# Expert stages: normalisation on ScalarE, bias additions behind the weighted row, and the first tile's work reordered

## The reference

```python
x = x + 0.5 * _L0_ffn_ref(_layernorm(x), gate_w, base_w, base_b, lora_A, lora_B)
x = x + _L0_attn_ref(_layernorm(x), wq, wk, wv, wo)
x = x + 0.5 * _L0_ffn_ref(_layernorm(x), gate_w, base_w, base_b, lora_A, lora_B)
x = x + 0.5 * _L1_ffn_ref(_layernorm(x), W_gate, W_up, W_down)       # SwiGLU
x = x + _L1_attn_ref(_layernorm(x), ...)                             # Mamba2
x = x + 0.5 * _L1_ffn_ref(_layernorm(x), W_gate, W_up, W_down)
```

```python
gate_logits = jnp.einsum('bsd,ed->bse', x, gate_w)            # 8 experts
weights, selected = jax.lax.top_k(gate_logits, 2)
weights = jax.nn.softmax(weights, axis=2)
result = jnp.einsum('bsd,od->bso', x, base_w) + base_b
w_full = jnp.sum(one_hot(selected, 8) * weights[..., None], axis=2)
low = jnp.einsum('bsd,erd->ebsr', x, lora_A)                  # rank 16
lora_out = jnp.einsum('ebsr,eor,bse->bso', low, lora_B, w_full)
return result + 2.0 * lora_out
```

## Time and profile before

| | us |
|---|---|
| median of 3 runs (2285.08 to 2288.72) | 2286.21 |
| the profiled execution | 2288.39 |
| its span in the profile | 2286.6 |
| first expert stage, to the first attention product | 0 to 80.1 |
| attention | 80.1 to 323.7 |
| second expert stage, to the first SwiGLU product | 323.7 to 384.3 |
| SwiGLU, Mamba2, SwiGLU | 384.3 to 2286.6 |
| TensorE, VectorE, ScalarE, GpSimd busy | 2165, 1704, 1416, 1045 |

### The profile page before, as it was taken

How to read it: one execution, slowest core, us unless ns; L and a number is a source line. 1 busy time by engine, 2 the same in 40 slices (tenths; PEclk the granted TensorE clock), 3 DMA queues, 4 the chain that set the end, 5 groups by cost and what they waited for, 6 DMA issues and landing times. The chain is left out here.

```text
span 2286.6 us, 34632 instructions
## 1 busy us (share of the span) xinstructions
PE 2165.4 (95%) x12541; PEld 1756.7 (77%) x12556; DVE 1703.8 (75%) x2693; ACT 1415.5 (62%) x3062; POOL 1045.4 (46%) x759
## 2 busy tenths in 40 slices
PE   6879978999999999999999999999999999997999
PEld 6756667888778878787887887887888788785887
DVE  7767767232688889889889889888988988986221
ACT  3267743333678776777767767776777677673332
POOL 4366544444144454435534634444544453455442
PEclk9899999999999999999999999999999999998999
DMA  3000010333233223322423323322332333231332
GB/s 129 1 1 1 1 42 24 93 92 92 85 137 107 97 84 139 120 84 84 143 88 111 106 96 113 120 84 99 128 116 84 113 114 116 84 108 39 94 93 83
DMA packets 64152, 202.52 MB, mean 89 GB/s; under 512 B 7024, under 2 KB 8048, under 8 KB 55664
## 3 DMA queue, kind: packets, MB, share of 16 engines
q1 hardware_dynamic: 63984, 200.31, 25.4%
HBM read 197.39 MB, written 2.88 MB: 88 GB/s over the span
## 5 line engine op out<-in xcount | busy, mean ns | idle before, releaser
L526 POOL TENSOR_TENSOR wAl<-rawA,wAh 128x512 fp32r<-128x512 f32 x233 | 326.9, 1415 | 411.2 <-ACT wAh L652 410.6
L1567 PE MATMUL ps<-xTh,wAh 128*128 128x512 f32 x1512 | 428.2, 405 | 7.4 <-DVE oacc L1397 3.0
L1567 PE MATMUL ps<-xTl,wAh 128*128 128x512 f32 x1512 | 417.1, 397 | 0.0
L1567 PE MATMUL ps<-xTh,wAl 128*128 128x512 f32 x1512 | 415.6, 396 | 0.0
L1292 DVE SCALAR_TENSOR_TENSOR work<-ps,chp,work 128x510 f32<-128x510 f32 (+2 forms) x465 | 343.3, 743 | 50.8 <-ACT work L804 40.7
L1567 PEld LDWEIGHTS ps<-xTl,wAh 128*128 128x128 f32 x1512 | 285.9, 189 | 70.0
L1567 PEld LDWEIGHTS ps<-xTh,wAl 128*128 128x128 f32 x1512 | 285.4, 189 | 69.8
L1567 PEld LDWEIGHTS ps<-xTh,wAh 128*128 128x128 f32 x1512 | 277.2, 189 | 78.3 <-issue 17.3
L532 POOL TENSOR_TENSOR wBl<-rawB,wBh 128x512 fp32r<-128x512 f32 x108 | 142.3, 1331 | 385.6 <-ACT wBh L656 385.6
L841 ACT ACTIVATE eb<-eb,gc 128x128 f32<-128x128 f32 x1008 | 307.7, 391 | 17.3 <-DMA eb<-scr_decays 17.3
L576 POOL TENSOR_TENSOR sqt<-gt 128x512 f32<-128x512 f32 x112 | 155.1, 1385 | 120.0 <-DVE gt L1351 112.1
(11 more groups left out here) (202 smaller groups left out, 3976.3 us busy)
## 6 DMA issues: line engine op xcount, KB each, us to landing
eb<-scr_decays SPq DMA_DIRECT2D x63, 1536.0 KB, 6.5
rawA<-ma_in SPq DMA_DIRECT2D x144, 256.0 KB, 3.7
rawA<-fa_in SPq DMA_DIRECT2D x88, 256.0 KB, 2.6
rawB<-mb_in SPq DMA_DIRECT2D x64, 256.0 KB, 2.9
rawB<-fb_in SPq DMA_DIRECT2D x44, 256.0 KB, 2.6
x<-x_in SPq DMA_DIRECT2D x8, 256.0 KB, 6.5
x_out<-x SPq DMA_DIRECT2D x8, 256.0 KB, 2.6
wqraw<-wqkv_in SPq DMA_DIRECT2D x1, 1536.0 KB, 11.1
```

The lines of the kernel that those rows point to most:

```text
L526: nc.gpsimd.tensor_tensor(wAl[:, slot, :], rawA[:, slot, :], wAh[:, slot, :].bitcast(F32), ALU.subtract).then_inc(A_lo, 1)
L1567: return nc.tensor.matmul(o, l, r, start=start, stop=end, **kw)
```

## The change

- In both expert stages the normalisation moves from VectorE to ScalarE. VectorE keeps `shift`, which writes minus mean times `brs` (one element a partition, L1085 of the new file) into `bsh`; ScalarE's `normalise` (L645) computes `brs` times x plus `bsh` with `Identity`. `SHIFTS` counts the shifts of the layers before. `last_norm` and the old `shift` become calls of these. Where VectorE still normalises later tiles itself (attention, SwiGLU), it first waits once for `ln_norm`.
- GpSimd's bias addition also waits for `l0_lw` of its tile, and so everything behind it does.
- First tile: VectorE takes the slices of `w0l` as their high parts come, with the statistics of tile 1 between the third and fourth; TensorE runs the first tile's passes against `w0h` and `w0l` slice by slice, and the transposes of tile 1 stand ahead of its last pass. The split of `lbl` on GpSimd waits for `w0_lo`. The attention's constants (`identb`, `negb`) are made in step 1 instead of ahead of the loop.

```diff
         for t in range(3):
             layer_rstd(0, t)
+        pool.wait_ge(w0_lo, KC)
         split_lo(0, lbl[:, :], lb_raw[:, :], lbh[:, :])
...
                     pool.wait_ge(ln_norm, 8 * k + t + 1)
+                    pool.wait_ge(l0_lw, 8 * i + t + 1)
                     nc.gpsimd.tensor_tensor(x[:, t, :], x[:, t, :], bh[:, :], ALU.add).then_inc(l0_bias, 1)
...
+        def normalise(k, t):
+            a, n = t % 2, 8 * k + t
+            act.wait_ge(ln_shift, SHIFTS[k] + t + 1)
+            if n >= 2:
+                act.wait_ge(ln_tp, n - 1)
+            nc.scalar.activation(work[:, a, :], x[:, t, :], ACT.Identity, bias=bsh[:, a:a + 1],
+                                 scale=brs[:, a:a + 1]).then_inc(ln_norm, 1)
...
+        w0_split(0)
+        normalise(0, 0)
+        w0_split(1)
+        layer_hi(0, 0, 1)
+        w0_split(2)
+        w0_split(3)
+        normalise(0, 1)
...
         def experts(i, k):
-            for t in range(-1, NT + AHEAD - 1):
-                if t + 1 < NT + AHEAD and (k, t) != (0, -1):
-                    layer_hi(*ln_tile(k, t + 1), 1)
+            if i == 1:
+                normalise(k, 0)
+                normalise(k, 1)
+                layer_hi(k, 0, 1)
+            for t in range(NT + AHEAD - 1):
+                layer_hi(*ln_tile(k, t + 1), 1)
+                if t + 2 < NT + AHEAD:
+                    normalise(*ln_tile(k, t + 2))
                 if 0 <= t - 1 < NT:
...
+                if i == 0 and t == 1:
+                    attention_constants()
...
+        def shift(k, t):
+            a, n = t % 2, 8 * k + t
+            dve.wait_ge(ln_rstd, n + 1)
+            if n >= 2:
+                dve.wait_ge(ln_norm, n - 1)
+            nc.vector.tensor_scalar(bsh[:, a:a + 1], bmv[:, a, 0:1], brs[:, a:a + 1], -1.0, ALU.mult,
+                                    ALU.mult).then_inc(ln_shift, 1)
...
+            def statistics(k, t):
+                if 8 * k + t >= 2:
+                    dve.wait_ge(ln_norm, 8 * k + t - 1)
+                layer_stats(k, t)
+
+            statistics(k, 0)
+            if i == 0:
+                shift(0, 0)
+                w0_rest(0)
+                w0_rest(1)
+                layer_lo(0, 0, 1)
+                w0_rest(2)
+                statistics(0, 1)
+                w0_rest(3)
+                shift(0, 1)
+            else:
+                statistics(k, 1)
+                shift(k, 0)
+                shift(k, 1)
+            statistics(k, 2)
+            if i == 1:
+                layer_lo(k, 0, 1)
+            for t in range(NT + AHEAD - 1):
+                if t + 2 < NT + AHEAD:
+                    shift(*ln_tile(k, t + 2))
+                layer_lo(*ln_tile(k, t + 1), 1)
+                if t + 3 < NT + AHEAD:
+                    statistics(*ln_tile(k, t + 3))
...
+                        if early and n < KC:
+                            pe.wait_ge(w0_hi, kc + 1)
+                        elif early and n < 2 * KC:
+                            pe.wait_ge(w0_lo, kc + 1)
+                        elif early and n == 2 * KC:
+                            pe.wait_ge(ln_lo, 1)
+                        if early and n == 2 * KC:
+                            layer_transpose(k, 1, 1, True)
```

More of the change, by code:

```diff
@@ L635, in layer_hi, with w0_split, attention_constants @@
                                  ACT.Copy).then_inc(ln_hi, 1)
-        for kc in range(KC):
+        def normalise(k, t):
[5 more added lines that the diff above has]
+                                 scale=brs[:, a:a + 1]).then_inc(ln_norm, 1)
+        def w0_split(kc):
             act.wait_ge(w0_s[kc], 16)
             nc.scalar.activation(w0h[:, kc, :], w0raw[:, kc, :], ACT.Copy).then_inc(w0_hi, 1)
-            if kc == 1:
-                layer_hi(0, 0, 1)
+        def attention_constants():
+            nc.scalar.activation(identb[:, :], ident, ACT.Copy).then_inc(act_step, 1)
+            for j in range(4):
+                nc.scalar.activation(negb[:, j, :], cst[:, C_NEG:C_NEG + P], ACT.Copy).then_inc(act_step, 1)
+        w0_split(0)
[5 more added lines that the diff above has]
+        normalise(0, 1)
         act.wait_ge(lb_s, 16)
         nc.scalar.activation(lbh[:, :], lb_raw[:, :], ACT.Copy).then_inc(wres_hi, 1)
-        act.wait_ge(cst_in_s, 16)
-        nc.scalar.activation(identb[:, :], ident, ACT.Copy).then_inc(act_step, 1)
-        for j in range(4):
-            nc.scalar.activation(negb[:, j, :], cst[:, C_NEG:C_NEG + P], ACT.Copy).then_inc(act_step, 1)
         def hi_A(n, g=0, per=0):
@@ L911, in step @@
                 hi_B(B0G + v + 2, g, TPG)
-        def last_norm(t):
-            a = t % 2
-            act.wait_ge(ln_shift, t + 1)
-            if t >= 2:
-                act.wait_ge(ln_tp, 8 * 5 + t - 1)
-            nc.scalar.activation(work[:, a, :], x[:, t, :], ACT.Identity, bias=bsh[:, a:a + 1],
-                                 scale=brs[:, a:a + 1]).then_inc(ln_norm, 1)
         def finish():
@@ L926, in finish @@
             y_hi(NG - 1, TPG - 1, 1)
-            last_norm(0)
+            normalise(5, 0)
             for t in range(1, AHEAD):
-                last_norm(t)
+                normalise(5, t)
                 layer_hi(5, t - 1, YBANK[(t - 1) % 2])
@@ L1081, in experts, with w0_rest @@
         def experts(i, k):
-            for t in range(-1, NT + AHEAD - 1):
-                if t == -1:
-                    layer_stats(k, 0)
-                    layer_stats(k, 1)
-                    layer_norm(k, 0)
-                    layer_stats(k, 2)
-                    layer_norm(k, 1)
-                    layer_lo(k, 0, 1)
-                    if i == 0:
-                        for kc in range(KC):
-                            dve.wait_ge(w0_hi, kc + 1)
-                            nc.vector.tensor_tensor(w0l[:, kc, :], w0raw[:, kc, :], w0h[:, kc, :].bitcast(F32),
-                                                    ALU.subtract).then_inc(w0_lo, 1)
-                else:
-                    if t + 1 < NT + AHEAD:
-                        layer_lo(*ln_tile(k, t + 1), 1)
-                    if t + 3 < NT + AHEAD:
-                        layer_stats(*ln_tile(k, t + 3))
-                    if t + 2 < NT + AHEAD:
-                        layer_norm(*ln_tile(k, t + 2))
+            def w0_rest(kc):
+                dve.wait_ge(w0_hi, kc + 1)
+                nc.vector.tensor_tensor(w0l[:, kc, :], w0raw[:, kc, :], w0h[:, kc, :].bitcast(F32),
+                                        ALU.subtract).then_inc(w0_lo, 1)
+            def statistics(k, t):
[25 more added lines that the diff above has]
+                    statistics(*ln_tile(k, t + 3))
                 if 0 <= t - 2 < NT:
@@ L1174, in attention @@
             dve.wait_ge(wres_lo, 9)
+            dve.wait_ge(ln_norm, 8 + AHEAD)
             layer_stats(1, AHEAD)
@@ L1233, in swiglu @@
             if i == 0:
+                dve.wait_ge(ln_norm, 8 * k + AHEAD)
                 layer_stats(k, AHEAD)
@@ L1397, in last_evacuate @@
             nc.vector.tensor_tensor(oacc[:, t, :], ps[:, FBANK[t], :], oacc[:, t, :], ALU.add).then_inc(m_osum, 1)
-        def shift(t):
-            a = t % 2
-            dve.wait_ge(ln_rstd, 8 * 5 + t + 1)
-            if t >= 2:
-                dve.wait_ge(ln_norm, 8 * 5 + t - 1)
-            nc.vector.tensor_scalar(bsh[:, a:a + 1], bmv[:, a, 0:1], brs[:, a:a + 1], -1.0, ALU.mult,
-                                    ALU.mult).then_inc(ln_shift, 1)
         def finish():
@@ L1419, in finish @@
                 if t >= 1:
-                    shift(t - 1)
+                    shift(5, t - 1)
                 if t >= 2:
@@ L1426, in finish @@
             last_evacuate(4)
-            shift(3)
+            shift(5, 3)
             layer_lo(5, 2, YBANK[0])
@@ L1610, in experts @@
             for t in range(-1, NT + AHEAD - 1):
-                if t + 1 < NT + AHEAD:
+                early = i == 0 and t == 0
+                if t + 1 < NT + AHEAD and not early:
                     layer_transpose(*ln_tile(k, t + 1), 1, True)
                 if 0 <= t < NT:
-                    if i == 0 and t == 0:
-                        pe.wait_ge(w0_lo, KC)
-                    pe.wait_ge(ln_lo, 8 * k + t + 1)
+                    if early:
+                        pe.wait_ge(ln_hi, 1)
+                    else:
+                        pe.wait_ge(ln_lo, 8 * k + t + 1)
                     if t >= 3:
```

2 lines of the change are left out of this document (1 added, 1 removed).

## The result

The changed kernel takes **2258.28 us** (median of four runs, 2256.16 to 2259.44) against 2287.47 us for the kernel before, timed beside it (2285.08 to 2289.0): a ratio of 0.9872, 95% interval 0.9855 to 0.9889. 29.2 us are gone, where 23.3 were forecast. The profiled execution has a span of 2253.9 us and took 2256.16.

The account below looks back on a forecast made before the run. VectorE was taken to bound the expert stages' steps, with TensorE the bound afterwards. Gains of 7.4 + 7.7 + 2.5 + 5.7 = 23.3 us off the median of 2286.2 gave 2262.9 us, range 2257 to 2270.

Parts of the forecast that it names:

- What bounds the kernel: Both expert stages: VectorE bound the steps, with 5.92 us of serial work against TensorE's 5.0.
- A, the steps: Second expert stage: VectorE's step falls to 4.3 us, TensorE's 5.0 decides; gain 4.5 us up to the ninth transposes.
- the start: Second expert stage's beginning: first product 0.4 us later, as the first normalisation passes through VectorE, ScalarE and TensorE.
- A, the end of the stage: Second stage, ninth transposes to first SwiGLU product: 8.9 us instead of 10.1, a gain of 1.2.
- B, the first tile: First stage's start: second tile's step at 17.0 us instead of 24.42, a gain of 7.4.
- C, the first stage: First stage's other steps: 4.4 us, then 5.0 each with two surcharges; 35.9 for 43.56, a gain of 7.7.
- The surcharge for `wqh`: First stage: `wqh` on ScalarE ahead of tile 4's high part delays TensorE's next products by 1.2 us.
- GpSimd's reach into the next tile: First stage, tiles 5 and 6: GpSimd's work lengthens VectorE's cast and L1126 by some 1.1 us each, hidden by TensorE.
- D, the end of the first stage: Last steps to first attention product: 9.6 us instead of 12.1, a gain of 2.5; GpSimd's clearing hidden.
- Rival 1: Expert steps: `shift` waits for GpSimd's bias addition, VectorE needs 5.5 us and stays the bound; 2269.8 us, chance 0.12.
- Rival 2: Steps stay at 5.9 and 6.2 us, as GpSimd's moved work slows other VectorE operations; 2275.5 us, chance 0.09.
- Rival 3: TensorE's clock stays low through both expert stages' 15 tiles, some 3 us more a step; slower, 2308 us, chance 0.02.

Follow-up runs that it names:

- e7_only_move: Changed kernel without GpSimd's bias wait and with the old first tile order, leaving little but the normalisation's move to ScalarE: 2281.56 us.
- e2_only_bias_wait: Kernel before plus only the wait putting GpSimd's bias addition behind VectorE's weighted row; normalisation stays on VectorE: 2278.80 us.
- e6_lora_low_first: As e5_quarter_splits, with the subtraction `lwTl` of tile 7 moved ahead of statistics and update of x on VectorE: 2260.51 us.
- e9_fill_e6: As e6_lora_low_first, with 18 unused matmuls added in TensorE's waits at each expert stage's end: 2255.53 us.
- e4_two_element_shift: Changed kernel with `shift` written over two elements of each partition in place of one: 2265.87 us.
- e3_old_first_tile: Changed kernel with the first tile's work put back into the old order: 2265.84 us.
- e5_quarter_splits: Changed kernel with ScalarE's `wqh` and `woh` cut into quarters over several steps and GpSimd's low halves one step earlier: 2256.55 us.
- e1_no_bias_wait: Changed kernel without the one wait that puts GpSimd's bias addition behind VectorE's weighted row: 2276.60 us.
- e8_fill_e5: As e5_quarter_splits, with 18 unused matmuls added in TensorE's waits at each expert stage's end: 2254.64 us.

## Why the prediction was right

**What bounds the kernel** held. VectorE led the steps, and with the change TensorE does: 33.50 us busy of 33.50.

**A, the steps.** 5.92 − 0.46 − 0.26 − 0.99 + 0.1 = 4.3 us of VectorE was to fall under TensorE's 5.0. Measured: VectorE is busy 29.27 of 33.50 us, about 4.3 a step, and in each step MAX8 waits some 0.3 us for TensorE, where before VectorE had no gap:

```profile
324.44 0.17 DVE L1159 MAX8 v<-ps 128x8 f32<-128x8 f32 x1 [0.29 <-PE ps L1599]
```

TensorE's own need was read 0.1 too large, 5.0 for 4.90; over the steps of the second stage that is 0.6 of the missing 0.8; the start, 0.24 later and not 0.4, is the rest. What the sum did not show is that its terms depend on each other. I had subtracted the normalisation (0.46) and the two waits (1.25) as three amounts; e7_only_move shows that without the wait the first is worth less than 0.1 us in a step, and e2_only_bias_wait that without the move part of the second comes back at the normalisation. The result was right because both were changed.

**A, the end of the stage** was the term most mis-sized: 7.77 us, not 8.9, and 2.1 more at the first SwiGLU products. I had priced that end with durations from the earlier trace rows, where the products after it take 2.05 us for four, the lower clock. After the change the clock is 1.00 there throughout. Three of the six missing microseconds are this. That part of the gain is luck, since nothing in the sum or in the change secures it: e6_lora_low_first and e9_fill_e6 show that it is the clock and that it can turn on how TensorE's idle time lies, and e4_two_element_shift, with the same waits as the changed kernel there, starts them at the lower clock all the same. The clock held in both traces of the changed kernel.

**B, the first tile** held closely: first product forecast at 9.6, measured at 9.61 (10.47 in the other trace of this kernel, which starts later as a whole); second tile's step at 17.0, measured at 16.55. The last 8 products take 1.43 us, the higher clock, which I had left open. e3_old_first_tile gives the part 7.5 us in the total.

**C, the first stage.** The surcharge for `wqh` was 1.2, as forecast: that step took 6.14 us, with the wait at 32.12 in it. One other step took 5.22, and the rest from the third tile on are again 4.9, not 5.0. The forecast's starts also hold a step of 5.3 (26.4 to 31.7) that its text gives no reason for; measured there: 4.94. GpSimd's reach into the next tile was forecast for tiles 5 and 6 and as hidden. It came for tiles 6 and 7 (L1162 with 1.07 us at 47.44, L1164 with 1.19 at 52.98), and for tile 7 it isn't hidden, since no further tile's products cover it: e5_quarter_splits takes 1.0 us out of that wait.

**D, the end of the first stage** was 8.89, not 9.6: tile 7's `lw` came at 55.08, about 3.4 us after its transposes, not 4.1. The clearing of `kBD` (3.52 us at 59.42) met nothing, as forecast; e4_two_element_shift shows what it would have cost had `shift` been two elements wide.

**The rivals.** Rival 1 (2269.8) fell: `shift` took 216 ns at most. But the reason I gave, that `shift` and the bias start from one event and overlap, was wrong: `shift` ends as the bias begins, and only two places test it. The Trainium skill (VectorE: DVE Perf Modes, "What auto-detection actually checks") lets the mode in for equal dimensions; the 0.22 us at 15.13 within GpSimd's split contradicts its use on this one-element instruction, while the 1.25 and 4.68 us of the two-element form follow it. Those agree with the Trainium skill (SBUF — State Buffer, "Who interferes with whom") too: held for the whole of GpSimd's instruction. Rival 2 (2275.5) fell: steps of 4.90. Rival 3, the clock as a loss, did not come within the steps (1.00 from 17 to 52 us and in the stretch above), but its mechanism works at the stages' ends and starts, with 1 to 3 us at a place. (The sum of rival 1 took 3.2 and 3.7 us for six and seven steps of 0.5; they make 3.0 and 3.5, so 2269.4 and not 2269.8.)

What stays open is what decides the clock at a stage's end: why it held at the changed kernel's second end but not at its first, and why it fell at the second end of e4_two_element_shift behind the same waits.

## What to carry to other kernels

When two engines exclude each other, don't price a removed instruction by its duration: find the loop that sets the step, and see whether the instruction lies in the part that the other engine covers. Here the move alone left the step at 5.8 to 5.9 us, the reordering alone gained 8.7 us in all, and the two together 21.7. Look at the engine that becomes the bound for idle pieces as well: what they cost may come after them, as a lower clock, and a reordering that only makes work earlier can lose by it (4.0 us here).

## What the runs showed of the hardware

- A VectorE `tensor_scalar` with immediate and pointer operands from one element a partition to one element ran in 0.22 us inside a GpSimd SBUF-to-SBUF subtraction; the same with two elements took 1.25 us there, and 4.68 us when GpSimd had a subtraction and a memset in a row. VectorE got no gap between GpSimd's two instructions there; in e1_no_bias_wait the cast did get one, between the bias addition (to 336.73) and the split (from 336.75).
- Such a wait shows as the duration of the waiting instruction, and its followers' too: behind the 4.68 us one, the subtraction `xTl`, which takes 0.68 us alone, is shown with 3.54.
- TensorE's granted clock fell to 0.50 (1.2 GHz) at the stage ends behind pieces in which the engine mostly waited. Matmuls without use, put into the waits, kept it at 1.00: by the traces 1.0 us gained in e8_fill_e5 and 4.5 in e9_fill_e6, where it had fallen before the SwiGLU products too. The waits alone do not tell where it falls: behind equal ones it stood at 1.00 in the changed kernel (354 to 358 us) and fell to 0.50 in e4_two_element_shift (from about 359).
